# Row tiles of 64 partitions for the first product of a fused adapter and feed-forward kernel

## The chip, the cores and the metric

The kernel runs on one core of a Trainium2 chip. The metric is the device time of one execution in microseconds (us); the kernel before takes 297.78 us, the median of 3 runs (297.61 to 297.8).

## What is computed

The reference, cut to what matters (x is 8 x 256 x 1024, the adapter weights 16 x 1024 x 1024, all fp32):

```
w = weight[adapter_ids]
y = einsum('bsi,boi->bso', x, w)             # first product, one adapter per batch row
t = y[:, perm] as 16 heads of 64
t = gelu(einsum('bhd,hdm->bhm', t, up))      # 64 -> 256
t = einsum('bhm,hmd->bhd', t, down)          # 256 -> 64
out = x + t[:, unperm]
```

## The kernel before

**Precision.** The operands of the first product and of `up` are split into a high part (rounded to the matmul's fp32r format by ScalarE) and a low part (the difference, by VectorE). Three products are added: high by high, high by low, low by high.

**The first product (unit g, 32 of them).** A unit is 256 output columns of one batch row: two halves `o` of 128 columns, each contracted over 8 steps `k` of 128 rows. One step is a matmul of 128 rows by 128 weights by 512 columns (L641: high weights by x's high and low part side by side, `x_pair`) and one of 256 columns (L645: low weights by x's high part). They go in four groups of four: L641 x4, L645 x4, and again. Each matmul is preceded by its own weight load. The 512 columns lie in one bank of PSUM: columns 0 to 255 are the sum with x's high part, 256 to 511 that with its low part, and VectorE adds the two (`y_sum`, L518, once per half `o`) into `y_out`, which is written to a scratch in HBM and gathered back by the permutation. Units 0 and 1 (`first_lora_piece`, L606 and L611) run in pieces as the first data land.

**`up` and `down`.** A feed-forward unit f (32 of them) is two heads. `up_unit` (L674, L677, L680) has 64 rows of contraction for each head, so it issues pairs: rows 0 to 63 to one bank, rows 64 to 127 to another, 12 such pairs of 64 rows by 128 weights by 512 columns in a unit (six for each `m`). `down_unit` (L698) has 128 rows and tiles of 64 columns.

**Order on TensorE.** Written out by hand. The 32 first-product units come in eight quads `q` of four. Behind quad 2 come two up units; behind quads 3 to 6 come two up units, four down units and two more up units; behind quad 7 the rest of up and down, alternating. So the engine goes from the first product to `up` six times (behind quads 2 to 7), and from `up` back to the first product five times (ahead of quads 3 to 7).

**Banks.** PSUM is four tensors `ps[0..3]` of two banks each. Two of them (a set) are used by two units of the first product, the other two by the next two; `up` takes a set too (`up_banks(f, m)`), so a unit waits for the GELU or the `y_sum` that empties its banks (`gelu_done`, `y_summed`).

**Supply.** ScalarE rounds the weights of unit g+2 (`w_high`, L381, two pieces of 1.06 us) once unit g is done, VectorE subtracts (`w_low`, L490, two of 1.22 us); SyncE loads four units ahead. ScalarE and VectorE work through lists in a fixed order, in which `y_sum`, `t_low`, `x_low` and `w_low` follow each other.

Of the kernel before, what the change touches and what calls it, by code (L numbers as in the profile page):

```python
# [10 lines left out]
ALU = mybir.AluOpType  # L11
ACT = mybir.ActivationFunctionType

P = 128
B, S, D = 8, 256, 1024
NW = 16
H, DH, M = 16, 64, 256
KT = D // P
OU = 256
OT = OU // P  # L20
# [5 lines left out]
FU = H // 2  # L26
MT = M // P
HALF = KT // 2
NL = B * LPB
NF = CH * FU  # L30

# [23 lines left out]
YS, TG, SS, HS, XR = 4, 6, 2, 4, 9  # L55
# [4 lines left out]
PAIR, QUAD, LEAD = 2, 4, 2  # L60
# [17 lines left out]
def build(nc, x_cols, x_rows, x_late, w, up, down, perm, ids, out_rows, out_late):  # L78
# [3 lines left out]
    with ctx:  # L82
# [14 lines left out]
        w_hi = sb("w_hi", [P, WS, KT, OU], F32R)  # L97
        w_lo = sb("w_lo", [P, WS, KT, OU], F32R)
# [62 lines left out]
        y_summed = sem("y_summed")  # L161
# [37 lines left out]
                return ps[2 * ((p // 2 + 1) % 2) + p % 2][:, f % 2, :]  # L199
            return ps[2 * ((p + 1 - TURNS + BLOCKS) % 2)][:, f % 2, :]  # L200

        def y_bank(g, o):
            q = g // QUAD
            return ps[2 * ((q + g % QUAD // 2 + (q == LEAD)) % 2) + g % 2][:, o, :].rearrange("p (c s) -> p c s", c=2)

        def token_parts(f):

# [278 lines left out]
        def _(dve):  # L486
# [26 lines left out]
            def y_sum(g):  # L513
                if g >= YS:
                    dve.wait_ge(y_parked[g % YS], 16 * (g // YS))
                for o in range(OT):
                    dve.wait_ge(lora_done, OT * g + o + 1)
                    nc.vector.tensor_reduce(y_out[:, g % YS, o, :], y_bank(g, o).rearrange("p c s -> p s c"),  # L518
                                            mybir.AxisListType.X, ALU.add).then_inc(y_summed, 1)

            def add_x(f):
# [70 lines left out]
        @block.tensor  # L592
        def _(pe):
            def warm():
                pe.wait_ge(ones_set, 1)
                for n in range(WARM):
                    nc.tensor.matmul(ps[3][:, 1, 0:P], ones, ones, start=True, stop=True)

            def first_lora_piece(g, n):
                ks = range(*FIRST[n])  # L600
                pe.wait_ge(first_x_lo, n + 1)
                pe.wait_ge(first_w_hi[g], n + 1)
                for o in range(OT):
                    col = slice(o * P, (o + 1) * P)
                    for k in ks:
                        nc.tensor.matmul(y_bank(g, o), w_hi[:, g, k, col], x_pair[:, 0, k, :, :], start=(k == 0), stop=False)  # L606
                pe.wait_ge(first_w_lo[g], n + 1)
                for o in range(OT):
                    col = slice(o * P, (o + 1) * P)
                    for k in ks:  # L610
                        last = nc.tensor.matmul(y_bank(g, o)[:, 0, :], w_lo[:, g, k, col], x_hi[:, 0, k, :], start=False, stop=(k == KT - 1))  # L611
                    if n == PIECES - 1:
                        last.then_inc(lora_done, 1)
                if g == 0 and n == HALF_PIECE:
                    last.then_inc(first_half_done, 1)

            def lora_unit(g):
                b, ws = g // LPB, g % WS
                xs = b % XS
                if g % LPB == 0:  # L620
                    pe.wait_ge(x_lo_done, b)


                q = g // QUAD
                if q > LEAD:
                    f = PAIR * 2 * (q - LEAD - 1) + g % QUAD // 2
                    pe.wait_ge(gelu_done, MT * f + g % 2 + 1)
                elif q == LEAD:
                    pe.wait_ge(y_summed, OT * (g - QUAD + 1))
                elif q > 0:  # L630
                    pe.wait_ge(y_summed, OT * (g - 1 if g % QUAD < 2 else g - 5))
                for o in range(OT):
                    col = slice(o * P, (o + 1) * P)
                    acc = y_bank(g, o)
                    for n in range(2):
                        ks = range(n * HALF, (n + 1) * HALF)

                        if o == 0:
                            pe.wait_ge(w_hi_done, 2 * (g - PAIR) + n + 1)
                        for k in ks:  # L640
                            nc.tensor.matmul(acc, w_hi[:, ws, k, col], x_pair[:, xs, k, :, :], start=(k == 0), stop=False)  # L641
                        if o == 0:
                            pe.wait_ge(w_lo_done, 2 * (g - PAIR) + n + 1)
                        for k in ks:
                            last = nc.tensor.matmul(acc[:, 0, :], w_lo[:, ws, k, col], x_hi[:, xs, k, :], start=False, stop=(k == KT - 1))  # L645
                    last.then_inc(lora_done, 1)

            def up_unit(f):
                p, ts = f // PAIR, f % SS

                behind_quad = p == 0 or p % 2 == 1 and p <= TURNS
                q = (p + 1) // 2 + LEAD
                if f == 0:
                    pe.wait_ge(up_lo_done, len(UP_UNITS))
                if behind_quad:

                    pe.wait_ge(y_summed, OT * (QUAD * q + 2 * (f % 2 + 1)))
                elif f % 2 == 1:

                    pe.wait_ge(added, f - 1 if p < TURNS else f - 3)  # L660
                pe.wait_ge(t_lo_done, f + 1)
                for m in range(MT):
                    col = slice(m * P, (m + 1) * P)


                    if not behind_quad and f % 2 == 0:
                        pe.wait_ge(gelu_done, MT * (f - 1) + m + 1)
                    if not behind_quad and f % 2 == 1 and p > TURNS:
                        pe.wait_ge(gelu_done, MT * (f - 3) + m + 1)
                    acc = up_banks(f, m)  # L670

                    for h in range(2):
                        own = slice(h * DH, (h + 1) * DH)
                        nc.tensor.matmul(acc[:, h, :], up_hi[own, f % FU, col], t_hi[own, ts, :], start=True, stop=False)  # L674
                    for h in range(2):
                        own = slice(h * DH, (h + 1) * DH)
                        nc.tensor.matmul(acc[:, h, :], up_hi[own, f % FU, col], t_lo[own, ts, :], start=False, stop=False)  # L677
                    for h in range(2):
                        own = slice(h * DH, (h + 1) * DH)
                        last = nc.tensor.matmul(acc[:, h, :], up_lo[own, f % FU, col], t_hi[own, ts, :], start=False, stop=True)  # L680
                    last.then_inc(up_done, 1)

            def down_unit(f):
                if f == 0:
                    pe.wait_ge(down_in, 16)

                p = f // PAIR
                if f % PAIR == 0:
                    if p < TURNS - 1:
                        pe.wait_ge(gelu_done, MT * PAIR * (p // 2 * 2 + 1) + p % 2 + 1)  # L690
                    else:
                        pe.wait_ge(gelu_done, MT * PAIR * (p + 1) + 1 if p + 1 < PAIRS else MT * NF)
                for n, tok in enumerate(token_parts(f)):
                    acc = down_place(f, n)
                    for m in range(MT):
                        pe.wait_ge(gelu_done, MT * f + m + 1)
                        for h in range(2):
                            last = nc.tensor.matmul(acc[h * DH:(h + 1) * DH, :], down_sb[:, 2 * (f % FU) + h, m, :],  # L698
                                                    hidden[:, f % HS, m, h, tok], start=(m == 0), stop=(m == MT - 1))
                    last.then_inc(down_done, 1)  # L700

            warm()
            for n in range(PIECES):
                for g in range(PAIR):
                    first_lora_piece(g, n)
            for q in range(QUADS):
                k = block_behind(q)
                for g in lora_of(q):
                    if g >= PAIR:
                        lora_unit(g)  # L710
                if k:
                    for f in units(2 * k - 1):
                        up_unit(f)
                    for f in units(2 * k - 2):
                        down_unit(f)
                    for f in units(2 * k - 1):
                        down_unit(f)
                if k is not None:
                    for f in units(2 * k):
                        up_unit(f)  # L720
            for p in range(TURNS, PAIRS):
                for f in units(p):
                    up_unit(f)
                for f in units(p - 1):
                    down_unit(f)
            for f in units(PAIRS - 1):
                down_unit(f)
# [37 lines left out]
```

## Time and profile before

| | |
|---|---|
| time, median of 3 runs | 297.78 us (297.61 to 297.8) |
| span of the profiled execution | 296.1 us |
| what lies around the span (the median less the span) | 1.7 us |
| TensorE matmul busy | 290.6 us, 98% |
| TensorE weight load busy | 215.0 us, 73% |
| VectorE, ScalarE, GpSimd busy | 61%, 54%, 33% |
| matmuls | 1694 |

The profiled execution has no time of its own beside its span, so the median of the runs stands for it. Busy time of TensorE counts overlapping matmuls once. The profiler's record of one matmul is longer than the slot it occupies (a matmul of 512 columns is recorded with 395 ns while the next starts 233 ns later), so what a matmul costs is read from start to start.

### The profile page before, as it was taken

What the parts mean: (1) busy time and instruction counts of PE and PEld (TensorE: products, weight loads), DVE (VectorE), ACT (ScalarE), POOL (GpSimd) and SP (SyncE); (2) the same over time, 40 slices, a digit from 0 to 9 for tenths busy, and PEclk for the clock granted to TensorE, in tenths of its full rate; (3) what the DMA queues carried; (4) which work ended last, traced back from release to release, by engine and by line L of the source; (5) the groups of instructions that cost most, each with busy time, mean ns of one, the idle gap of its engine ahead of it and who ended that gap; (6) DMA issues with size and microseconds to landing.
All of it is one profiled execution on the core that took longest, in us unless ns stands there. A gap on an engine that the chain in (4) does not pass through costs nothing.

```text
span 296.1 us, 4358 instructions
## 1 busy us (share of the span) xinstructions
PE 290.6 (98%) x1694; PEld 215.0 (73%) x1694; DVE 179.2 (61%) x211; ACT 159.9 (54%) x179; POOL 98.8 (33%) x92
## 2 busy tenths in 40 slices
PE   8999999999999999999999999999999999999994
PEld 7788888888888838886488855888468885444441
DVE  3599679589778455973658726685446523343333
ACT  5655453466764368344584265822853207777750
POOL 4000000068552007860527007702473405222234
PEclk9999999999999999999999999999999999999999
DMA  7999999999988947799576973876752864421335
GB/s 206 363 402 421 395 421 422 366 320 375 394 328 277 378 153 197 281 360 406 212 249 196 345 311 114 312 237 199 244 191 83 286 185 122 128 71 71 144 142 212
DMA packets 23699, 77.87 MB, mean 263 GB/s; under 512 B 2688, under 2 KB 11264, under 8 KB 18816
## 3 DMA queue, kind: packets, MB, share of 16 engines
q1 hardware_dynamic: 7056, 43.39, 39.3%
q0 software_dynamic: 7488, 25.18, 24.7%
q10 hardware_dynamic: 9136, 9.05, 8.8%
q8 instruction: 13, 0.21, 0.3%
q14 instruction: 6, 0.05, 0.1%
HBM read 60.82 MB, written 16.78 MB: 262 GB/s over the span
## 4 chain that ended last, share of the span: by engine, by line
PE 95%; DMA 2%; SPq 1%; POOL 1%; issue 0%; DVE 0%; ACT 0%; POOLq 0%; DVEq 0%
PE ps L641 38%; PE ps L645 19%; PE ps L698 19%; PE ps L674 6%; PE ps L677 5%; PE ps L680 5%; PE ps L606 2%; DMA w_raw<-w 2%; PE ps L611 1%; POOL out_late L319 1%; SPq L223 1%; SPq L251 0%; DVE w_raw L528 0%; ACT w_hi L429 0%; POOLq L361 0%
## 5 line engine op out<-in xcount | busy, mean ns | idle before, releaser
L641 PE MATMUL ps<-x_pair,w_hi 128*128 128x512 f32 x480 | 131.5, 395 | 0.0
L381 ACT ACTIVATE w_hi<-w_raw 128x1024 fp32r<-128x1024 f32 x58 | 58.3, 1056 | 62.8 <-PE ps L645 51.6
L415 ACT ACTIVATE hidden<-ps 128x1024 f32<-128x1024 f32 x64 | 61.6, 1028 | 55.1 <-PE ps L680 47.1
L641 PEld LDWEIGHTS ps<-x_pair,w_hi 128*128 128x128 f32 x480 | 82.0, 189 | 12.8 <-issue 1.8
L645 PEld LDWEIGHTS ps<-x_pair,w_lo 128*128 128x128 f32 x480 | 73.6, 189 | 10.2
L490 DVE TENSOR_TENSOR w_lo<-w_raw,w_hi 128x1024 fp32r<-128x1024 f32 x60 | 71.0, 1222 | 11.8 <-ACT w_hi L381 10.7
L645 PE MATMUL ps<-x_pair,w_lo 128*128 128x256 f32 x480 | 76.3, 281 | 0.0
L292 POOL DMA_INDIRECT t_raw<-y_rows,idx x32 | 34.9, 1090 | 115.1 <-DMA y_rows<-y_out 82.4
L518 DVE TENSOR_REDUCE y_out<-ps 128x256 f32<-128x512 f32 x64 | 42.8, 685 | 24.5 <-PE ps L645 23.0
L698 PE MATMUL ps<-hidden,down_sb 128*64 128x512 f32 (+1 forms) x264 | 57.4, 583 | 0.0
L510 DVE TENSOR_TENSOR t_lo<-t_raw,t_hi 128x512 fp32r<-128x512 f32 x32 | 21.7, 694 | 47.9 <-ACT t_hi L405 42.5
L698 PEld LDWEIGHTS ps<-hidden,down_sb 128*64 128x64 f32 x264 | 18.0, 137 | 34.0 <-issue 30.9
L298 POOL DMA_INDIRECT rows<-x_rows,idx x16 | 22.6, 1414 | 14.7 <-PE ps L645 10.8
L674 PE MATMUL ps<-t_hi,up_hi 64*128 64x512 f32 x128 | 27.0, 418 | 0.0
L311 POOL DMA_INDIRECT out_rows<-rows,idx x16 | 20.1, 1254 | 18.2 <-DVE rows L528 14.9
L677 PE MATMUL ps<-t_lo,up_hi 64*128 64x512 f32 x128 | 25.1, 389 | 0.0
L680 PE MATMUL ps<-t_hi,up_lo 64*128 64x512 f32 x128 | 25.0, 387 | 0.0
L405 ACT ACTIVATE t_hi<-t_raw 128x512 fp32r<-128x512 f32 x32 | 19.9, 642 | 0.9 <-DMA t_raw<-y_rows,idx 0.9
L674 PEld LDWEIGHTS ps<-t_hi,up_hi 64*128 64x128 f32 x128 | 12.0, 184 | 11.4 <-issue 7.3
L499 DVE TENSOR_TENSOR x_pair<-x_raw,x_pair 128x2048 fp32r<-128x2048 f32 x7 | 16.0, 2292 | 4.9 <-ACT x_pair L387 4.7
L528 DVE TENSOR_TENSOR rows<-ps,rows 128x512 f32<-128x512 f32 x16 | 11.0, 690 | 10.3 <-PE ps L698 10.3
L307 POOL DMA_INDIRECT w_raw<-x_late,idx x8 | 8.3, 1042 | 23.1 <-DVE w_lo L490 17.0
(29 smaller groups left out, 119.4 us busy)
## 6 DMA issues: line engine op xcount, KB each, us to landing
w_raw<-w SPq DMA_DIRECT2D x29, 1024.0 KB
y_rows<-y_out ACTq DMA_DIRECT2D x32, 256.0 KB
x_raw<-x_cols SPq DMA_DIRECT2D x7, 1024.0 KB
w_raw<-w SPq DMA_DIRECT2D x4, 256.0 KB, 5.0
w_raw<-w SPq DMA_DIRECT2D x2, 512.0 KB, 7.7
hidden<-up SPq DMA_DIRECT2D x1, 1024.0 KB, 12.3
down_sb<-down SPq DMA_DIRECT2D x1, 1024.0 KB, 12.3
w_raw<-w SPq DMA_DIRECT2D x2, 384.0 KB, 6.9
```

Source lines behind the costliest of these rows:

```text
L292: nc.gpsimd.indirect_dma_start(t_raw[:, f % TG, :], None, y_rows[0:D * (chunk + 1), :], rows_of(f)).then_inc(t_in[f % TG], 16)
L298: nc.gpsimd.indirect_dma_start(row_place(f), None, x_rows, rows_of(f)).then_inc(rows_in[f % XR], 16)
L381: nc.scalar.activation(w_hi[:, g % WS, k, :], w_raw[:, g % WRAW, k, :], ACT.Copy).then_inc(w_hi_done, 1)
L415: nc.scalar.activation(hidden[:, f % HS, m, :, :], up_banks(f, m)[:, :, :], ACT.Gelu).then_inc(gelu_done, 1)
L490: nc.vector.tensor_tensor(w_lo[:, g % WS, k, :], w_raw[:, g % WRAW, k, :], w_hi[:, g % WS, k, :].bitcast(F32), ALU.subtract).then_inc(w_lo ...
L518: nc.vector.tensor_reduce(y_out[:, g % YS, o, :], y_bank(g, o).rearrange("p c s -> p s c"), mybir.AxisListType.X, ALU.add).then_inc(y_summ ...
L641: nc.tensor.matmul(acc, w_hi[:, ws, k, col], x_pair[:, xs, k, :, :], start=(k == 0), stop=False)
L645: last = nc.tensor.matmul(acc[:, 0, :], w_lo[:, ws, k, col], x_hi[:, xs, k, :], start=False, stop=(k == KT - 1))
L674: nc.tensor.matmul(acc[:, h, :], up_hi[own, f % FU, col], t_hi[own, ts, :], start=True, stop=False)
L677: nc.tensor.matmul(acc[:, h, :], up_hi[own, f % FU, col], t_lo[own, ts, :], start=False, stop=False)
L680: last = nc.tensor.matmul(acc[:, h, :], up_lo[own, f % FU, col], t_hi[own, ts, :], start=False, stop=True)
L698: last = nc.tensor.matmul(acc[h * DH:(h + 1) * DH, :], down_sb[:, 2 * (f % FU) + h, m, :], hidden[:, f % HS, m, h, tok], start=(m == 0), s ...
```

## The change

For units 2 to 31 each step of 128 rows becomes two row tiles of 64 rows, as in `up`, each with its own bank. To fit two banks per half unit, x's high and low part are no longer side by side but two matmuls of 256 columns that accumulate into the same columns. A step has then six matmuls of 64 rows by 128 weights by 256 columns (three pairs), each with a weight load, in place of one of 512 and one of 256 columns. VectorE now adds the two row tiles rather than the high and the low sum. Where both halves `o` of a unit share the two banks (units that are not `by_half`), `y_sum` is one instruction over 1024 elements after the whole unit; where each half has banks of its own and two units share those (`by_half`: the last two units of quads 3 to 7), it stays one per half. The waits of `lora_unit` and `up_unit` follow the new places.

```
-        def y_bank(g, o):
+        def by_half(g):
+            return g // QUAD > LEAD and g % QUAD >= PAIR
+        def y_tiles(g, o):
+            n, m = (o, g % 2) if by_half(g) else (g % 2, o)
+            return ps[2 * y_set(g) + n][:, :, m * S:(m + 1) * S]
...
             def y_sum(g):
...
+                if g >= PAIR and not by_half(g):
+                    dve.wait_ge(lora_done, OT * (g + 1))
+                    nc.vector.tensor_reduce(y_out[:, g % YS, :, :].rearrange("p o s -> p (o s)"),
+                                            ps[2 * y_set(g) + g % 2][:, :, :].rearrange("p r t -> p t r"),
+                                            mybir.AxisListType.X, ALU.add).then_inc(y_summed, OT)
+                    return
...
             def lora_unit(g):
...
+                    if by_half(g):
+                        if g % 2 == 0:
+                            pe.wait_ge(gelu_done, MT * f + o + 1)
+                        else:
+                            pe.wait_ge(y_summed, OT * (g - 1) + o + 1)
...
                         for k in ks:
-                            nc.tensor.matmul(acc, w_hi[:, ws, k, col], x_pair[:, xs, k, :, :], start=(k == 0), stop=False)
+                            for c in range(2):
+                                for r in range(2):
+                                    own = slice(r * ROWS, (r + 1) * ROWS)
+                                    nc.tensor.matmul(acc[:, r, :], w_hi[own, ws, k, col], x_pair[own, xs, k, c, :],
+                                                     start=(k == 0 and c == 0), stop=False)
...
                         for k in ks:
-                            last = nc.tensor.matmul(acc[:, 0, :], w_lo[:, ws, k, col], x_hi[:, xs, k, :], start=False, stop=(k == KT - 1))
+                            for r in range(2):
+                                own = slice(r * ROWS, (r + 1) * ROWS)
+                                last = nc.tensor.matmul(acc[:, r, :], w_lo[own, ws, k, col], x_hi[own, xs, k, :],
+                                                        start=False, stop=(k == KT - 1))
...
             def up_unit(f):
...
-                if behind_quad:
-                    pe.wait_ge(y_summed, OT * (QUAD * q + 2 * (f % 2 + 1)))
+                if behind_quad and f % 2 == 0:
+                    pe.wait_ge(y_summed, OT * (QUAD * q + PAIR))
+                elif behind_quad:
+                    pass
...
+                    if behind_quad and f % 2 == 1:
+                        pe.wait_ge(y_summed, OT * (QUAD * q + 3) + m + 1 if q > LEAD else OT * (QUAD * q + 3 + m))
```

## Rows read from the trace of the kernel before

**Rows 1.** The page: busy shares, granted clock, chain of work that ended last.

```profile
span 296.1 us, 4358 instructions
PE 290.6 (98%) x1694; PEld 215.0 (73%) x1694; DVE 179.2 (61%) x211; ACT 159.9 (54%) x179; POOL 98.8 (33%) x92
...
PEclk9999999999999999999999999999999999999999
...
PE ps L641 38%; PE ps L645 19%; PE ps L698 19%; PE ps L674 6%; PE ps L677 5%; PE ps L680 5%; PE ps L606 2%; DMA w_raw<-w 2%; PE ps L611 1%; POOL out_late L319 1%; SPq L223 1%; SPq L251 0%; DVE w_raw L528 0%; ACT w_hi L429 0%; POOLq L361 0%
```

**Rows 2.** The page's groups: line engine op, shapes, count | busy us, mean ns.

```profile
L641 PE MATMUL ps<-x_pair,w_hi 128*128 128x512 f32 x480 | 131.5, 395 | 0.0
L645 PE MATMUL ps<-x_pair,w_lo 128*128 128x256 f32 x480 | 76.3, 281 | 0.0
```

**Rows 3.** Waits, all engines: who waited for whom, us, times, longest.

```profile
ACT w_hi L381 <- PE ps L645: 51.6, 18, 3.6
...
ACT w_hi L381 <- DMA w_raw<-w: 1.7, 2, 1.0
...
PE ps L597 <- DVE rows L543: 1.1, 1, 1.1
...
PE ps L606 <- ACT w_hi L429: 0.4, 1, 0.4
```

**Rows 4.** Chain in order of time, one unit apart (start us, us).

```profile
119.30 0.93 PE ps L641 x4
...
124.91 0.93 PE ps L641 x4
```

**Rows 5.** Timeline of PE from the first product into up (start us, us).

```profile
98.56 0.63 PE L645 MATMUL ps<-x_pair,w_lo 128*128 128x256 f32 x4
99.03 1.09 PE L641 MATMUL ps<-x_pair,w_hi 128*128 128x512 f32 x4
99.96 0.64 PE L645 MATMUL ps<-x_pair,w_lo 128*128 128x256 f32 x4
100.52 0.50 PE L674 MATMUL ps<-t_hi,up_hi 64*128 64x512 f32 x2
100.86 0.40 PE L677 MATMUL ps<-t_lo,up_hi 64*128 64x512 f32 x2
```

**Rows 6.** Timeline of PE from up into the first product.

```profile
110.82 0.40 PE L677 MATMUL ps<-t_lo,up_hi 64*128 64x512 f32 x2
...
113.11 0.39 PE L680 MATMUL ps<-t_hi,up_lo 64*128 64x512 f32 x2
113.43 1.20 PE L641 MATMUL ps<-x_pair,w_hi 128*128 128x512 f32 x4
114.47 0.39 PE L645 MATMUL ps<-x_pair,w_lo 128*128 128x256 f32 x2
```

**Rows 7.** Timeline after a wait in up: weight loads (PEld) and matmuls (PE).

```profile
250.76 0.19 PEld L674 LDWEIGHTS ps<-t_hi,up_hi 64*128 64x128 f32 x2 [0.32 <-DVE w_raw L528]
250.76 0.50 PE L674 MATMUL ps<-t_hi,up_hi 64*128 64x512 f32 x2
250.87 0.19 PEld L677 LDWEIGHTS ps<-t_lo,up_hi 64*128 64x128 f32 x2
```

**Rows 8.** Timeline of weight loads beside the matmuls of rows 5.

```profile
98.91 0.54 PEld L641 LDWEIGHTS ps<-x_pair,w_hi 128*128 128x128 f32 x3
```

**Rows 9.** Timeline at the first matmul of unit 0, behind a wait.

```profile
6.09 0.19 PEld L606 LDWEIGHTS ps<-x_pair,w_hi 128*128 128x128 f32 x1 [0.26 <-DVE x_pair L534]
6.12 0.47 PE L606 MATMUL ps<-x_pair,w_hi 128*128 128x512 f32 x1
```

**Rows 10.** TensorE's sequencer at line L696, window 101 to 105 us (min/median/max ns).

```profile
L696 PEldq EVENT_SEMAPHORE  x2: 51/728/1406, 101.5 to 103.5; - x2
```

**Rows 11.** Timeline of VectorE in units 13 to 15, and PE into unit 15.

```profile
90.26 1.28 DVE L518 TENSOR_REDUCE y_out<-ps 128x256 f32<-128x512 f32 x2
91.46 2.34 DVE L490 TENSOR_TENSOR w_lo<-w_raw,w_hi 128x1024 fp32r<-128x1024 f32 x2
93.72 0.68 DVE L518 TENSOR_REDUCE y_out<-ps 128x256 f32<-128x512 f32 x1
...
94.34 0.64 PE L645 MATMUL ps<-x_pair,w_lo 128*128 128x256 f32 x4
94.82 0.63 PE L641 MATMUL ps<-x_pair,w_hi 128*128 128x512 f32 x2
```

More of the change, by code:

```diff
@@ L28 @@
 HALF = KT // 2
+ROWS = P // 2
 NL = B * LPB
@@ L200, in down_bank, with y_set, first_bank @@
             return ps[2 * ((p + 1 - TURNS + BLOCKS) % 2)][:, f % 2, :]
-        def y_bank(g, o):
+        def y_set(g):
             q = g // QUAD
-            return ps[2 * ((q + g % QUAD // 2 + (q == LEAD)) % 2) + g % 2][:, o, :].rearrange("p (c s) -> p c s", c=2)
+            return (q + g % QUAD // 2 + (q == LEAD)) % 2
+        def by_half(g):
+            return g // QUAD > LEAD and g % QUAD >= PAIR
+        def first_bank(g, o):
+            return ps[2 * y_set(g) + g % 2][:, o, :].rearrange("p (c s) -> p c s", c=2)
+        def y_tiles(g, o):
+            n, m = (o, g % 2) if by_half(g) else (g % 2, o)
+            return ps[2 * y_set(g) + n][:, :, m * S:(m + 1) * S]
         def token_parts(f):
@@ L515, in y_sum @@
                     dve.wait_ge(y_parked[g % YS], 16 * (g // YS))
+                if g >= PAIR and not by_half(g):
[4 more added lines that the diff above has]
+                    return
                 for o in range(OT):
+                    parts = first_bank(g, o) if g < PAIR else y_tiles(g, o)
                     dve.wait_ge(lora_done, OT * g + o + 1)
-                    nc.vector.tensor_reduce(y_out[:, g % YS, o, :], y_bank(g, o).rearrange("p c s -> p s c"),
+                    nc.vector.tensor_reduce(y_out[:, g % YS, o, :], parts.rearrange("p c s -> p s c"),
                                             mybir.AxisListType.X, ALU.add).then_inc(y_summed, 1)
@@ L605, in first_lora_piece @@
                     for k in ks:
-                        nc.tensor.matmul(y_bank(g, o), w_hi[:, g, k, col], x_pair[:, 0, k, :, :], start=(k == 0), stop=False)
+                        nc.tensor.matmul(first_bank(g, o), w_hi[:, g, k, col], x_pair[:, 0, k, :, :], start=(k == 0), stop=False)
                 pe.wait_ge(first_w_lo[g], n + 1)
@@ L610, in first_lora_piece @@
                     for k in ks:
-                        last = nc.tensor.matmul(y_bank(g, o)[:, 0, :], w_lo[:, g, k, col], x_hi[:, 0, k, :], start=False, stop=(k == KT - 1))
+                        last = nc.tensor.matmul(first_bank(g, o)[:, 0, :], w_lo[:, g, k, col], x_hi[:, 0, k, :], start=False, stop=(k == KT - 1))
                     if n == PIECES - 1:
@@ L624, in lora_unit @@
                 q = g // QUAD
-                if q > LEAD:
-                    f = PAIR * 2 * (q - LEAD - 1) + g % QUAD // 2
+                f = PAIR * 2 * (q - LEAD - 1) + g % QUAD // 2
+                if q > LEAD and not by_half(g):
                     pe.wait_ge(gelu_done, MT * f + g % 2 + 1)
@@ L629, in lora_unit @@
                     pe.wait_ge(y_summed, OT * (g - QUAD + 1))
-                elif q > 0:
+                elif 0 < q < LEAD:
                     pe.wait_ge(y_summed, OT * (g - 1 if g % QUAD < 2 else g - 5))
@@ L633, in lora_unit @@
                     col = slice(o * P, (o + 1) * P)
-                    acc = y_bank(g, o)
+                    acc = y_tiles(g, o)
+                    if by_half(g):
[3 more added lines that the diff above has]
+                            pe.wait_ge(y_summed, OT * (g - 1) + o + 1)
                     for n in range(2):
```

## The prediction

> **What bounds the kernel now.** The page comes first. Matmuls are busy for 98% of the span at the full granted clock (all slices show 9 and over, the 2.4 GHz level), and the chain of work that ended last lies on TensorE for 95%: 38% of it on L641 and 19% on L645, the two matmuls of the changed units [rows 1]. Then the waits: TensorE waited for other engines only 1.1 and 0.4 us, both at the start, while ScalarE waited 51.6 us for the first product and only 1.7 us for weights from DMA [rows 3]. So every ns of a TensorE slot counts in full, and supply follows TensorE. The groups give 480 steps (30 units x 2 halves x 8) [rows 2]. The price of a step is read from start to start: a unit takes 124.91 - 119.30 = 5.61 us in the chain [rows 4], that is 16 steps of 0.3508 us. It splits into 0.93 / 4 = 0.2325 us for 512 columns and 0.47 / 4 = 0.1175 for 256 [rows 5].
>
> **What the change takes away: changes of tile shape.** The first product has 128-row tiles, `up` 64-row tiles. Into `up`, four L645 take 100.52 - 99.96 = 0.56 us where they take 0.47 within a unit, and the first pair then takes 100.86 - 100.52 = 0.34 where the later ones take 0.23: 0.09 + 0.11 = 0.20 us [rows 5, 6]. Back again, the last pair takes 113.43 - 113.11 = 0.32 (0.09 more) and four L641 take 114.47 - 113.43 = 1.04 (0.11 more): 0.20 us too [rows 6]. After the change both have tiles of 64 rows and 128 columns. Six changes into `up` and five back go, one comes new between unit 1 and unit 2: 10 x 0.20 = 2.0 us less, all on TensorE's path, since there is nothing that it then waits for (below). The shapes of `down` stay and so do their costs. TensorEngine Tiling (Array Packing), Key Properties, in the Trainium skill says that a change of the tiling mode drains the array; by that the 0.09 goes in any case, and the trace agrees.
>
> **What the change reprices: the step.** It removes a 512-column and a 256-column matmul and adds three pairs of 64 rows by 256 columns; matmuls go from 1694 to 1694 + 4 x 480 = 3614. No row shows a 64-row pair of 256 columns. The nearest are these.
> - The 64-row pair of 512 columns in `up`: from 110.82 to 113.11 us there are ten pairs, 0.229 us each [rows 6]. Its two matmuls start together and run side by side: one slot for two. Against 0.2325 for one 128-row matmul of 512 columns it is 1.5% shorter.
> - The 128-row matmul of 256 columns: 0.1175 [rows 5].
>
> Lower bound: half of 0.229, 0.1145 us, if a pair costs by its columns alone. Then a step is 0.3435, 0.0073 less, x 480 = 3.5 us less. A floor under it is the weight load: behind a wait the next loads start 0.11 us after the first [rows 7], so no slot goes below 0.11 (0.33 a step, 10.0 us less); I see no reason to get there, since the 256-column slot of now, with one such load, is 0.1175 and not 0.11.
> Upper bound: a pair has two weight loads and two matmuls, four instructions in a slot, twice what any stretch of before needs. After the one kind of wait that empties the queue, a matmul follows its load 0.03 us later (6.09, 6.12) [rows 9]. If that is the pace of handing out instructions, a slot is 4 x 0.03 = 0.12 us, a step 0.36, 0.0092 more, x 480 = 4.4 us more.
> Value taken: 0.117, the present 256-column slot less most of the 1.5% that row pairs save at 512 columns, since length is the same and only the rows differ. A step is 0.351: x 480 = 0.1 us more, so nothing. Splitting the 512 columns gives back what pairs save.
>
> **Could the two weight loads in a slot be one after the other?** That would be 0.22 us a slot and is excluded: after a wait both loads of a pair and both matmuls start at 250.76, and the next pair of loads starts at 250.87, as long as one load takes [rows 7].
>
> **Weight loads and matmuls overlap already.** The timeline shows L641's loads starting at 98.91, while L645 still runs, and one slot apart after that [rows 8, 5]. TensorE: Matmul & The Clock Gate, Part 3, in the Trainium skill says that a weight load overlaps a running matmul only when its row group differs. By that rule the 128-row stream would pay each load in full, and a change to two row tiles would save far more than I count: 0.11 us for each of 960 loads, over 100 us. Here the trace is against it, and it gets no chance: 0.1175 us for 256 columns leaves no room for an exposed load of 0.11.
>
> **VectorE and the waits that move.** `y_sum` of a whole unit is one instruction in place of two, which took 1.28 us together when run one after the other [rows 11]; I count about 1.2 for the one. It starts only after the whole unit, so the sum lands about 0.5 us later than the second half's did. Behind it stand `w_low` of two units ahead and, on ScalarE, the store of `y_out` with the next `w_high`: both have a unit of 5.6 us. The tight one is new: the first half of unit 15 waits until VectorE has summed the first half of unit 14, since they share banks. That sum ends at 93.72 + 0.68 = 94.40 and unit 15 begins at 94.82 [rows 11]: 0.42 us of cover. Quad 3 starts 0.20 us sooner, and VectorE's list ahead of it shortens by 0.1: cover 0.3, cost 0. With slots of 0.1145 the three units before it shorten by 0.35 us more and the cover is just gone, for 0.1 us, once. In later quads VectorE is further ahead. DMA needs no more than now, and ScalarE waits for it 1.7 us in all [rows 3].
>
> **Sum.** 297.8 (the median of the runs; span 296.1, around it 1.7) + 0.1 - 2.0 = 295.9 us, 0.6% faster. About 0.2% is what a measurement of this kernel can tell from no change, 0.6 us.
>
> **Rivals.**
> - *Instructions are handed out too slowly* (the other side). The price is above: 297.8 + 4.4 - 2.0 = 300.2 us. It decides from the point where it eats 2.0 us: a step of 0.355, a slot of 0.1183, 0.0296 us an instruction. For it: the 0.03 of [rows 9]. Against it: at L696 the sequencer's wait that began at 101.5 us and took 1.406 us ended at 102.9, and its next wait, two down units and so 32 instructions further if it is the one ahead of f = 2, began at 103.5: 0.6 / 32 = 0.019 us each [rows 10]. But the trace doesn't name which instruction that wait stands ahead of. Chance 0.20. TensorE: Matmul & The Clock Gate, Part 1, in the Trainium skill gives about 62 ns for a matmul where hardware decoding is off and a floor of 25 ns where it is on; by the first, an estimate, a slot would be 0.124, a step 0.372 and the time 306 us; no row shows which holds.
> - *Row pairs lose something at 256 columns*: two loads of 0.11 us, a few ns apart, have to fit a slot of 0.117, and any slip shows. Slot 0.119 to 0.120: 1.9 us and more, less 2.0; 298 to 300 us. For it: no stretch of before has loads that dense. Chance 0.15.
> - *Cost by columns alone*, a slot of 0.1145: 297.8 - 3.5 - 2.0 + 0.1 = 292.4 us. For it: pairs are shorter at 512 columns than single matmuls. Against it: 256 columns now cost 0.1175, more than half of 0.2325. Chance 0.20.
> - *TensorE starts to wait* for `y_sum` or GELU, 0.3 us in each of five quads, 1.5 us: 297.4 us. Chance 0.05.
>
> The forecast has 0.40: slots of 0.1155 to 0.1183, 293.6 to 297.8 us. Range over the cases: 292.2 to 302.2 us, which takes in both bounds of the slot and leaves out some 0.08 on either side. Faster by over 0.2%: 0.20 of the columns case, 0.29 of the forecast's: 0.49. Within 0.2%: 0.17 (the forecast's upper end, waits, part of the denser loads). Slower: 0.34.
>
> **What would show it.** The start-to-start time of pairs in a unit (0.117; 0.12 or more says hand-out or loads, 0.1145 says columns); the last slot before `up` and the first in it like any other (else the 2.0 us are wrong); TensorE's waits still near 1.5 us in all; a single `y_sum` of about 1.2 us. The prediction fails most easily by the slot: 0.001 us in it is 1.4 us of time.

## The result, and the profile after

The changed kernel takes 300.31 us (median of 4 runs, 299.84 to 300.7) beside 297.69 us for the kernel before (4 runs, 297.53 to 297.8): a ratio of 1.0085, 95% interval 1.0071 to 1.0099. It is 0.85% slower; the forecast was 295.9 us, faster. The profiled execution took 299.84 us, the shortest of the four, and has a span of 298.0 us. In this document medians take in all runs of a kernel, while ratios leave out the runs more than 1.5% above its fastest (two of six of v1, five of twelve of v3).

The page of the kernel after, its busy shares and its chain, answers to [rows 1]:

```profile
span 298.0 us, 8180 instructions
PE 292.2 (98%) x3614; PEld 240.2 (81%) x3614; DVE 177.0 (59%) x191; ACT 159.9 (54%) x179; POOL 100.9 (34%) x92
...
PEclk9999999999999999999999999999999999999999
...
PE ps L673 39%; PE ps L680 19%; PE ps L739 18%; PE ps L715 5%; PE ps L718 5%; PE ps L721 5%; PE ps L629 3%; PE ps L634 1%; DMA w_raw<-w 1%; DVE w_raw L551 1%; POOL out_late L335 1%; SPq L239 1%; ACT w_hi L445 0%; POOLq L377 0%; SPq L267 0%
```

TensorE is as full as before, at the same granted clock, and the same two products set the end. Its busy time has grown by 1.6 us. So the loss is in how long TensorE takes for the work, not in waits. TensorE's waits confirm it (who waited for whom, us, times, longest), as in [rows 3]:

```profile
PE ps L620 <- DVE rows L566: 1.1, 1, 1.1
...
PE ps L629 <- ACT w_hi L445: 0.7, 1, 0.7
```

The chain in order of time (start us, us) shows the step; it answers to [rows 4]:

```profile
114.33 0.95 PE ps L673 x16
115.28 0.48 PE ps L680 x8
...
120.08 0.96 PE ps L673 x16
```

A unit takes 120.08 - 114.33 = 5.75 us (the next one 5.76), 16 steps of 0.360 us, where it was 0.3508. Eight pairs take 0.96, so a pair's slot is 0.120 us. That is 480 x (0.360 - 0.3508) = 4.4 us more.

TensorE's timeline from the first product into `up` and back, in the kernel after, answers to [rows 5] and [rows 6]:

```profile
100.98 0.64 PE L680 MATMUL ps<-x_pair,w_lo 64*128 64x256 f32 x8
101.46 0.40 PE L715 MATMUL ps<-t_hi,up_hi 64*128 64x512 f32 x2
101.69 0.40 PE L718 MATMUL ps<-t_lo,up_hi 64*128 64x512 f32 x2
...
113.94 0.39 PE L721 MATMUL ps<-t_hi,up_lo 64*128 64x512 f32 x2
114.17 1.11 PE L673 MATMUL ps<-x_pair,w_hi 64*128 64x256 f32 x16
115.12 0.64 PE L680 MATMUL ps<-x_pair,w_lo 64*128 64x256 f32 x8
```

The last four pairs of a unit take 101.46 - 100.98 = 0.48 us, like any other, and the first `up` pair 0.23, where they took 0.56 and 0.34. Back again, the last `up` pair takes 0.23 in place of 0.32 and the first eight pairs 0.95, no more than later ones. Nothing of either seam is left. So both 0.20 us costs are gone: ten changes, 2.0 us.

4.4 - 2.0 = 2.4 us more; the medians differ by 2.6, and the wait for `w_hi` at the start has grown by 0.3. The spans of the two traces differ by 1.9 only, since the start took less in this execution: unit 2 begins at 17.98 us, in the kernel before at 18.70. The quads show the account without it: each of quads 3 to 7 takes 23.03 us in place of 22.64, and 64 steps at 0.0092 more, less the 0.20 of two half seams, are 0.39.

VectorE at units 13 to 15 (timeline) answers to [rows 11]:

```profile
90.79 1.22 DVE L534 TENSOR_REDUCE y_out<-ps 128x512 f32<-128x1024 f32 x1
...
94.19 0.68 DVE L541 TENSOR_REDUCE y_out<-ps 128x256 f32<-128x512 f32 x1
```

And TensorE into unit 15:

```profile
95.70 1.12 PE L673 MATMUL ps<-x_pair,w_hi 64*128 64x256 f32 x16
```

The one-instruction sum takes 1.22 us. The sum that unit 15 waits for ends at 94.19 + 0.68 = 94.87, so the new wait has 95.70 - 94.87 = 0.83 us of cover: more than thought, because TensorE is later.

### The profile page after: what moved, and what is told of

Read it like the earlier page. It is cut to its first block, busy times and chain, and to the rows that moved or that the text cites. A ratio compares the mean times of both kernels' runs of the same rounds, so it can differ in the third digit from the quotient of the medians.

```text
span 298.0 us, 8180 instructions
## 1 busy us (share of the span) xinstructions
PE 292.2 (98%) x3614; PEld 240.2 (81%) x3614; DVE 177.0 (59%) x191; ACT 159.9 (54%) x179; POOL 100.9 (34%) x92
## 4 chain that ended last, share of the span: by engine, by line
PE 95%; DMA 1%; DVE 1%; POOL 1%; SPq 1%; issue 0%; ACT 0%; POOLq 0%; DVEq 0%
PE ps L673 39%; PE ps L680 19%; PE ps L739 18%; PE ps L715 5%; PE ps L718 5%; PE ps L721 5%; PE ps L629 3%; PE ps L634 1%; DMA w_raw<-w 1%; DVE w_raw L551 1%; POOL out_late L335 1%; SPq L239 1%; ACT w_hi L445 0%; POOLq L377 0%; SPq L267 0%
## 5 line engine op out<-in xcount | busy, mean ns | idle before, releaser
L673 PE MATMUL ps<-x_pair,w_hi 64*128 64x256 f32 x1920 | 134.9, 280 | 0.0
L673 PEld LDWEIGHTS ps<-x_pair,w_hi 64*128 64x128 f32 x1920 | 124.0, 188 | 0.5
L680 PE MATMUL ps<-x_pair,w_lo 64*128 64x256 f32 x960 | 77.2, 280 | 0.0
L308 POOL DMA_INDIRECT t_raw<-y_rows,idx x32 | 35.5, 1108 | 116.9 <-DMA y_rows<-y_out 101.4
L680 PEld LDWEIGHTS ps<-x_pair,w_lo 64*128 64x128 f32 x960 | 66.1, 188 | 0.0
L534 DVE TENSOR_REDUCE y_out<-ps 128x512 f32<-128x1024 f32 x20 | 24.4, 1221 | 17.0 <-PE ps L680 17.0
L314 POOL DMA_INDIRECT rows<-x_rows,idx x16 | 24.3, 1518 | 13.3 <-PE ps L680 9.1
L541 DVE TENSOR_REDUCE y_out<-ps 128x256 f32<-128x512 f32 x24 | 16.2, 687 | 18.3 <-PE ps L680 18.3
L715 PE MATMUL ps<-t_hi,up_hi 64*128 64x512 f32 x128 | 26.3, 407 | 0.1
```

Source lines behind the costliest of these rows:

```text
L308: nc.gpsimd.indirect_dma_start(t_raw[:, f % TG, :], None, y_rows[0:D * (chunk + 1), :], rows_of(f)).then_inc(t_in[f % TG], 16)
L314: nc.gpsimd.indirect_dma_start(row_place(f), None, x_rows, rows_of(f)).then_inc(rows_in[f % XR], 16)
L534: nc.vector.tensor_reduce(y_out[:, g % YS, :, :].rearrange("p o s -> p (o s)"), ps[2 * y_set(g) + g % 2][:, :, :].rearrange("p r t -> p t r"),
L673: nc.tensor.matmul(acc[:, r, :], w_hi[own, ws, k, col], x_pair[own, xs, k, c, :], start=(k == 0 and c == 0), stop=False)
L680: last = nc.tensor.matmul(acc[:, r, :], w_lo[own, ws, k, col], x_hi[own, xs, k, :], start=False, stop=(k == KT - 1))
```

## The experiments

What needs a cause is the slot: why 0.120 us for 256 columns, and is it the split, the row tiles, the weight loads or the number of instructions?

### e1, e2, e3: fewer columns, shorter loads, both

From the kernel after. e1 has 192 moving columns instead of 256, e2 weight loads of 64 columns instead of 128, e3 both; the edit of e3:

```diff
-nc.tensor.matmul(acc[:, r, :], w_hi[own, ws, k, col], x_pair[own, xs, k, c, :],
+few = slice(0, S if k == 0 and c == 0 else 192)
+part = slice(o * P, o * P + (P if k == 0 and c == 0 else 64))
+out = slice(0, P if k == 0 and c == 0 else 64)
+nc.tensor.matmul(acc[out, r, few], w_hi[own, ws, k, part], x_pair[own, xs, k, c, few],
...
-last = nc.tensor.matmul(acc[:, r, :], w_lo[own, ws, k, col], x_hi[own, xs, k, :],
+wide, much = (P, S) if k == KT - 1 else (64, 192)
+last = nc.tensor.matmul(acc[0:wide, r, 0:much], w_lo[own, ws, k, o * P:o * P + wide], x_hi[own, xs, k, 0:much],
```

> The changed kernel with 192 of the 256 columns in all matmuls of the first product in units 2 to 31, except each half unit's first high pair and last low pair (left out: the other columns' work). Theory A, the slot of a pair is set by its weight loads (load start to next matmul 0.117 us, plus 0.003): the slot stays 0.120 us and the time near 300 us. Theory B, instructions are handed out every 0.03 us: 0.120 as well. Theory C, the columns of a row pair set it: 0.120 x 192 / 256 = 0.090 us, and about 1260 slots x 0.030 = 38 us less.

> The changed kernel with weight loads of 64 instead of 128 columns in the same matmuls, 256 moving columns (left out: half of the output columns). Theory A (loads): a load is half as long (about 0.053 us less), so the slot falls to what 256 columns need by themselves, about 0.1145 us (half of a 512-column pair's 0.229), minus nothing else; two changes of tile shape per half unit come on top. Theory B (hand-out, four instructions in a slot): 0.120 still. Theory C (columns): 0.120 still.

> Both at once: weight loads of 64 columns and 192 moving columns, still two loads and two matmuls in a slot. Theory A (loads) and C (columns): about 0.086 to 0.090 us. Theory B (hand-out at 0.03 us an instruction): the slot can't go below 0.120. This run decides B.

Their times of one run each (316.27, 308.99 and 301.45 us, beside 297.56 for the kernel before) say little about the slot, for in all three TensorE stood still in places and its granted clock fell. In e1 these pauses are 4.1 us in `up` and 7.5 us in 21 pieces inside the first product. In e1, the page's slices of the granted clock:

```profile
PEclk9999999997789999988999999979999999999999
```

and TensorE's timeline in `up` behind quad 2:

```profile
77.03 0.79 PE L719 MATMUL ps<-t_hi,up_hi 64*128 64x512 f32 x2 [4.14 <-issue]
77.59 0.66 PE L722 MATMUL ps<-t_lo,up_hi 64*128 64x512 f32 x2
78.02 0.66 PE L725 MATMUL ps<-t_hi,up_lo 64*128 64x512 f32 x2
```

TensorE had stood still for 4.1 us, and then a pair of 512 columns takes 78.02 - 77.59 = 0.43 us in place of 0.23: the lower level, 1.2 GHz, until 81.4 us. `up` had come early for its rows: TensorE was through with the first product at 72.9 us, 2 us sooner than in the kernel before, and ScalarE's `t_hi` waited for the gathering DMA until 75.53 us. TensorE ran ahead of what feeds it and paid twice.

The slot is read from an undisturbed stretch. TensorE's timelines, e1 first:

```profile
169.68 1.13 PE L676 MATMUL ps<-x_pair,w_hi 64*128 64x192 f32 x16
170.57 0.71 PE L684 MATMUL ps<-x_pair,w_lo 64*128 64x192 f32 x8
```

Then e2:

```profile
168.36 1.09 PE L676 MATMUL ps<-x_pair,w_hi 64*64 64x256 f32 x16
169.27 0.65 PE L684 MATMUL ps<-x_pair,w_lo 64*64 64x256 f32 x8
```

And e3:

```profile
169.58 0.88 PE L676 MATMUL ps<-x_pair,w_hi 64*64 64x192 f32 x16
170.30 0.57 PE L684 MATMUL ps<-x_pair,w_lo 64*64 64x192 f32 x8
```

Eight pairs take 0.89 us in e1 (0.111 a slot), 0.91 in e2 (0.114) and 0.72 in e3 (0.090). With fewer columns the slot stops at 0.111, the time of one 128-column load in [rows 7]; with shorter loads it stops at 0.114, half of an `up` pair of 512 columns (0.229); with both it goes to 0.090. There are four instructions in each of these slots, so one can be handed out every 0.0225 us or faster, in a stretch of this length. The rival "instructions are handed out too slowly" needed 0.03 and falls. What is left is odd: 0.111 with full loads, 0.114 with all columns, but 0.120 where both are full length.

### e5: loads of 96 columns

The edit is that of e2 with 96 for 64.

> The changed kernel with weight loads of 96 of 128 columns, except each half unit's first high and last low pair (left out: a quarter of the output columns). Theory D: 0.1067 + 96 x 0.000104 = 0.1167 us a slot (0.120 at 128, 0.1135 at 64). If a load costs a fixed time whatever its length, 0.120.

303.75 us, one run, beside 297.76. TensorE's timeline:

```profile
83.16 1.09 PE L675 MATMUL ps<-x_pair,w_hi 64*128 64x256 f32 x16
84.09 0.63 PE L683 MATMUL ps<-x_pair,w_lo 64*96 64x256 f32 x8
```

The eight pairs of the first row take 0.93 us, a slot of 0.116 (the first pair has full loads, the row names only that form). That lies between the 0.114 of 64 columns and the 0.120 of 128. So a load costs a little of a slot long before it would fill it. The expectation for a cost that grows with the load's length was 0.1167, and for a fixed one 0.120; the first came near. The total says nothing of it, since the trace has 2.3 us of pauses inside the first product.

### e8: the split alone, in the kernel before

```diff
-nc.tensor.matmul(acc, w_hi[:, ws, k, col], x_pair[:, xs, k, :, :], start=(k == 0), stop=False)
+for c in range(2):
+    nc.tensor.matmul(acc[:, c, :], w_hi[:, ws, k, col], x_pair[:, xs, k, c, :],
+                     start=(k == 0 and c == 0), stop=False)
```

> The kernel before with one thing of the change alone: L641 split into two 128-row matmuls of 256 columns (x's high and low part), each with its own weight load, into the columns they had. Theory D (a fixed cost for each load): a step is 3 x 0.1175 to 3 x 0.120 = 0.3525 to 0.360 us, so 298.5 to 302.1 us, and the split rather than the row tiles makes the change slow. Theory E (row pairs are the cause): 0.3508 and 297.7 us.

303.01 us (302.71 to 303.51, 4 runs), ratio 1.0165, interval 1.0114 to 1.0215. Its chain:

```profile
119.01 0.96 PE ps L642 x8
...
120.45 0.96 PE ps L642 x8
```

Matmuls of all 128 rows, one load and one matmul to a slot, and the slot is 0.120 us again (0.96 / 8). The step is (120.45 - 119.01) / 4 = 0.360, so the split costs 480 x 0.0092 = 4.4 us with no row tile in the program. It has the costs of tile shapes as well, since it still changes between 128 and 64 rows, and its list of waits has one of 0.6 us that the kernel before has not (L646 for `w_lo`).

297.76 + 4.4 + 0.6 = 302.8, measured 303.01. And the kernel after is 2.7 us faster than this one: 2.6 of it are the 2.0 us of the ten changes and that wait. This run decides: the slot of 0.120 belongs to 256-column matmuls in a row, not to pairs.

### v1: row tiles without the split

The complement. Pairs of 512 columns and of 256, as L641 and L645 were; each half of a unit then has four parts in two banks, and `y_sum` adds four parts:

```diff
-for c in range(2):
-    for r in range(2):
-        own = slice(r * ROWS, (r + 1) * ROWS)
-        nc.tensor.matmul(acc[:, r, :], w_hi[own, ws, k, col], x_pair[own, xs, k, c, :],
-                         start=(k == 0 and c == 0), stop=False)
+for r in range(2):
+    own = slice(r * ROWS, (r + 1) * ROWS)
+    nc.tensor.matmul(acc[:, r, :], w_hi[own, ws, k, col], x_pair[own, xs, k, :, :],
+                     start=(k == 0), stop=False)
...
+nc.vector.tensor_reduce(y_out[:, g % YS, o, :], y_tiles(g, o).rearrange("p r (c s) -> p s r c", c=2),
+                        mybir.AxisListType.XY, ALU.add).then_inc(y_summed, 1)
```

> Row tiles without the split: the high product as pairs of 512 columns (x's high and low part side by side), the low product as pairs of 256, two banks for each half unit, so a unit takes a whole set of four banks and y_sum adds four parts. Theory D (a slot costs its columns, 1 / 2.4 GHz each, plus what its weight loads take from it, 0.013 us for loads of 128 columns, however many columns move): a step is 0.229 + 0.120 = 0.349 us against 0.3508, 480 x 0.0018 = 0.9 us less, with the ten changes of tile shape saved (2.0 us) 294.8 us, plus whatever TensorE waits for y_sum, which is twice the work on VectorE. Theory E (a 64-row pair of 256 columns is slow in itself or the saved changes of shape were never saved): 297.7 or slower.

302.89 us (300.29 to 305.24, 6 runs), ratio 1.0114, interval 1.0058 to 1.0170. TensorE's timeline inside a quad:

```profile
124.11 1.09 PE L658 MATMUL ps<-x_pair,w_hi 64*128 64x512 f32 x8
...
125.51 1.09 PE L658 MATMUL ps<-x_pair,w_hi 64*128 64x512 f32 x8
```

Four steps take 125.51 - 124.11 = 1.40 us, a step of 0.350: that of the kernel before, with twice the instructions. Row pairs neither save nor cost anything in a slot. The 0.229 us of a pair in `up` is not 1.5% that pairs save at 512 columns, as the prediction had it. The changes of tile shape are saved here too: three of quads 3 to 7 take 22.43 to 22.48 us where all took 22.64.

The run still lost 4.8 us of span, outside the slots, where the expectation was 294.8 us. The largest part, 1.75 us, is `up` behind quad 2, where VectorE is late with its longer sums; TensorE stands still for 1.2 us twice, the second time by this wait:

```profile
PE ps L700 <- DVE y_out L534: 1.2, 1, 1.2
```

Quads 4 and 6 take 22.87 and 23.63 us, with pauses inside them. At the start and late in the run there is another 1.6 us. The rest is at the seam behind a quad:

```profile
211.82 1.22 DVE L534 TENSOR_REDUCE y_out<-ps 128x256 f32<-128x1024 f32 x1 [1.23 <-PE ps L665]
213.55 1.94 ACT L427 ACTIVATE hidden<-ps 128x1024 f32<-128x1024 f32 x2 [5.53 <-DVE y_out L534]
213.87 0.40 PE L706 MATMUL ps<-t_hi,up_lo 64*128 64x512 f32 x2
214.63 0.65 PE L724 MATMUL ps<-hidden,down_sb 128*64 128x512 f32 x2 [0.35 <-ACT hidden L427]
```

The sum of half a unit takes 1.22 us in place of 0.68; ScalarE's GELU stands in its program behind the store of that sum, and `down` starts 214.63 - 213.87 = 0.76 us after the last `up` pair, not 0.32 as in the kernel before. The `up` stretches behind quads 3 to 7 take 3.01 to 3.59 us in place of 2.94.

### v2, v3: a candidate from these two

If the split is the loss and the tile shapes the gain, row pairs of full width in units 12 to 31 alone should keep the gain and spare VectorE in the crowded first part. v3 also moves one store on ScalarE:

```diff
 for f in units(2 * k - 1):
     gelu(f)
+    if f % 2 == 0:
+        y_park(QUAD * q + 3)
     t_high(f + PAIR)
```

> The kernel before, with row tiles of 64 rows for units 12 to 31 alone (the quads between two up stretches) and without the split: one pair of 512 columns and one of 256 a step, four banks of parts, summed by VectorE in two instructions of 1.22 us. Units 2 to 11 stay as before. Theory (the split cost the 4.4 us, the tile shapes give 0.20 us at each change, VectorE's longer sums eat part of it): quads at 22.43 us as in the undisturbed ones of the version with row pairs everywhere, where they were 22.64 before; up stretches behind them 3.00 instead of 2.94 because the last sum comes late; up stretches ahead of them 2.85. Per quad 0.24 us less, less up to 0.1 where down then waits for GELU; five quads: 0.7 to 1.2 us, so 296.5 to 297.1 us beside 297.7. Rival (VectorE's doubled sums are felt in every quad): quads or up stretches 0.4 us and more longer, 298.5 us and more.

> The same kernel with one instruction moved on ScalarE: the store of the last y_out of a quad comes behind the first GELU of the up stretch instead of ahead of it, so that GELU does not wait until VectorE has summed that unit. Theory: TensorE's down stretch behind that up stretch starts as early as in the kernel before (0.315 us between the last up matmul and the first down matmul or less, where the version with row pairs everywhere once took 0.756), 0.1 to 0.4 us in each of up to five quads: 295.7 to 296.9 us. Rival (ScalarE has slack there and the wait is VectorE's alone): same time as the kernel without the move, within 0.2 us.

v2: 299.47 us (298.32 to 302.25, 9 runs), ratio 1.0068, interval 1.0038 to 1.0097. v3: 300.7 us (296.72 to 303.33, 12 runs), ratio 1.0024, interval 0.9989 to 1.0058. v2 is slower than the kernel before, by 0.7%, and v3 is not shown to be faster; both missed their expectations, and v2 landed where its rival had it. In v2 `up` behind quads 3 to 7 takes 3.58, 3.12, 3.04, 3.26 and 3.01 us where it took 2.94; with the moved store, in v3, it takes 2.96, 2.94, 2.86, 3.01 and 3.01, so that part is cured. The spread of v3 is not the clock: the granted clock was 0.994 to 1.0 in all twelve runs. Its traced execution took 301.64 us, one of the longer ones. Its timeline of TensorE shows that the mechanism is there all the same:

```profile
172.26 0.63 PE L668 MATMUL ps<-x_pair,w_lo 64*128 64x256 f32 x8
172.74 0.40 PE L704 MATMUL ps<-t_hi,up_hi 64*128 64x512 f32 x2
172.97 0.40 PE L707 MATMUL ps<-t_lo,up_hi 64*128 64x512 f32 x2
...
175.28 0.39 PE L710 MATMUL ps<-t_hi,up_lo 64*128 64x512 f32 x2
175.59 0.65 PE L728 MATMUL ps<-hidden,down_sb 128*64 128x512 f32 x2
```

The slots at the seam are 0.48 / 4 and 0.23 us, none is long, and `down` follows the last `up` pair after 0.31 us. Two stretches of first product between `up` and `up` (span, busy time of PE, PEld, DVE, ACT and POOL; the last three columns are granted clock, DMA share, GB/s) show what spoils it:

```profile
113.39:137.50 24.11, 23.32 (x259) 22.14 (x257) 19.07 (x17) 10.87 (x12) 15.12 (x13) 1.00 0.90 316
150.31:172.74 22.43, 22.43 (x260) 19.60 (x257) 18.62 (x17) 10.85 (x12) 6.71 (x6) 1.00 0.83 259
```

The second quad takes 22.43 us against 22.64 before, the first 24.11. The third takes 24.72, and TensorE's timeline of it has such a place:

```profile
190.41 0.51 PE L668 MATMUL ps<-x_pair,w_lo 64*128 64x256 f32 x4 [0.84 <-issue]
```

In the middle of a run of eight (the first four start at 189.17), where the program waits for nothing, TensorE stands still ("issue": nothing that the profile shows). Instruction records of the DMA queues lie close by in time, and the kernel moves 0.29 MB of instructions where the one before moves 0.21; but the kernel after moves 0.46 MB and has no such pause. The cause stays open.

### e4, e7, e6: what a load costs in other places

e4 is the kernel before with L645 over 128 of its 256 columns; e7 is the kernel before with loads of 64 columns; e6 is v1 with loads of 64 columns. The edit of e4:

```diff
-last = nc.tensor.matmul(acc[:, 0, :], w_lo[:, ws, k, col], x_hi[:, xs, k, :], ...)
+last = nc.tensor.matmul(acc[:, 0, 0:P], w_lo[:, ws, k, col], x_hi[:, xs, k, 0:P], ...)
```

> The kernel before with the low product (L645) over 128 of its 256 columns (left out: half of that product). Theory A (loads): the 128-row slot of 256 columns is already set by its load, so with 128 columns it hardly falls, 0.115 to 0.118 us, and the time stays within 1 to 2 us of 297.7. Theory C (columns): 0.1175 falls to about 0.06 us, 960 slots... that is 480 x 0.058 = 28 us less. Theory B says nothing here (two instructions in a slot, 0.06 at least): also about 28 us less.

293.82 us, one run, beside 297.56. TensorE's timeline:

```profile
82.99 0.56 PE L645 MATMUL ps<-x_pair,w_lo 128*128 128x128 f32 x4
...
84.35 0.56 PE L645 MATMUL ps<-x_pair,w_lo 128*128 128x128 f32 x4
```

Four steps take 84.35 - 82.99 = 1.36 us (1.367 in the median of the trace), 0.340 to 0.342 a step against 0.3508. Half the columns of L645 save 0.01 us of a step, not the 0.06 that columns alone would: there is a floor under a slot with a 128-column load, near the 0.11 us of [rows 7]. In the trace the second to fourth of these slots take 0.110 to 0.113 us; the first takes 0.058, and the 512-column slot behind the four takes 0.05 more than it did.

> The kernel before with weight loads of 64 columns instead of 128 in L641 and L645 of the units from two on, except for the first of the eight hi steps and the last of the eight lo steps; half of the output columns get no sum of these steps. If the 256-column slot of a single 128-row matmul is set by its 128-column load, it falls from 0.118 towards the 0.1135 that pairs of 256 columns took with 64-column loads, and the 512-column slot stays at 0.2325: a step 0.005 us less, 2 us in all. If columns alone set it, nothing changes, 297.6 us.

297.03 us, one run, beside 297.81. A step becomes shorter:

```profile
82.48 1.08 PE L642 MATMUL ps<-x_pair,w_hi 128*64 128x512 f32 x4
...
85.24 1.08 PE L642 MATMUL ps<-x_pair,w_hi 128*64 128x512 f32 x4
```

(85.24 - 82.48) / 8 = 0.345 us, about 0.006 less, 2.8 us in 480 steps; but the time fell by 0.8 only. A wait of 1.4 us came up that was not there, in `up` for the sum of y (L676 for `y_out`); what is left of the difference one run can't settle.

> The variant with pairs of 512 columns, with weight loads of 64 columns (left out: half of the output columns). Theory D: the 512-column pair falls from 0.226 to 0.229 to 0.213 + 0.007 = 0.220 us, the 256-column pair to 0.1135. If the cost goes with the moving columns, the 512-column pair loses twice what the 256-column pair lost (0.0065): 0.213 to 0.216.

303.97 us, one run, beside 297.76; the total is again made by waits and pauses elsewhere. The timeline gives the step:

```profile
123.89 1.08 PE L659 MATMUL ps<-x_pair,w_hi 64*64 64x512 f32 x8
...
125.28 1.08 PE L659 MATMUL ps<-x_pair,w_hi 64*128 64x512 f32 x8
...
126.66 0.62 PE L659 MATMUL ps<-x_pair,w_hi 64*64 64x512 f32 x4
```

Eight steps take 126.66 - 123.89 = 2.77 us, 0.346 a step (0.345 in the median of the trace), as in e7 and 0.005 less than v1. Pairs and single matmuls gain the same from shorter loads. The 512-column slot falls to some 0.230 us in both runs, not to the 0.220 that was expected of e6: the rule that fitted 256 columns does not hold for 512.

So where long and short matmuls stand side by side, halving the loads saves some 0.003 us a slot, and the load is felt most where every slot is 256 columns: 0.006, from 0.120 to 0.114.

### v4: hi and lo by turns

The last experiment uses that. Only the order in the second half of each unit changes:

```diff
 for k in ks:
     nc.tensor.matmul(acc, w_hi[:, ws, k, col], x_pair[:, xs, k, :, :], start=(k == 0), stop=False)
+    if o == 1:
+        last = nc.tensor.matmul(acc[:, 0, :], w_lo[:, ws, k, col], x_hi[:, xs, k, :], ...)
+if o == 1:
+    continue
```

> The kernel before, with the matmuls of each unit's second half in another order: hi and lo by turns (512, 256, 512, 256 columns) in place of four of 512 and four of 256. Same instructions, same tiles, same sums; the first halves stay. In the kernel before, a slot's length depends on its neighbours: the fourth 512-column slot of a run, which the load of a 256-column matmul follows, takes 228.7 ns on the mean of 61 runs and the others 231.8 to 239.2; the first 256-column slot behind them takes 117.0 and the later ones 118.9 to 120. Theory (a slot costs by its neighbours, so loads that stand next to a 512-column matmul are hidden better): a step by turns is 0.2287 + 0.117 = 0.3457 us where it is 0.3508 now; 240 steps save 1.2 us, 296.6 us beside 297.7. Rival (the slots' spread is only the bookkeeping of one run of four, and the sum stays 0.3508): no change, 297.4 to 298.0 us. A third (loads of 256-column slots hidden worse when each follows a long one): slower.

297.17 us (12 runs, 296.95 to 298.3) beside 297.82 (17 runs), ratio 0.9974, interval 0.9949 to 1.0000. By its median it is the fastest version that leaves nothing out, by 0.26%, at the edge of what can be told. The chain, four steps by turns and four of the old order:

```profile
121.37 0.23 PE ps L641
121.60 0.12 PE ps L643
...
124.15 0.92 PE ps L641 x4
...
125.55 0.93 PE ps L641 x4
```

Eight steps by turns take 124.15 - 121.37 = 2.78 us, 0.3475 a step, against 1.40 / 4 = 0.350 in the old order: 240 x 0.0025 = 0.6 us, about what was measured and half of what was expected. In the median of the trace a 256-column slot by turns is 0.1165 us, as reckoned, but a 512-column slot is 0.231 and not 0.2287. Each of quads 3 to 7 takes 22.55 us where it took 22.64.

## Why the prediction was wrong, step by step

- **The step that failed is the value taken for the slot: "Value taken: 0.117 ... so nothing."** It measures 0.120, and 480 x 3 x 0.003 = 4.3 us is the whole error. Three readings lay behind it. First, 0.1175 was read from one group of four L645 of the kernel before. Its chain in order of time shows two kinds by turns:

```profile
120.23 0.47 PE ps L645 x4
...
121.63 0.48 PE ps L645 x4
```

That is 0.119 on the mean of the two, and the prediction's own step says 0.3508 - 0.2325 = 0.1183. Second, such a slot stands in a run of four between 512-column ones, whose first slot is short (0.117, the later ones 0.118 to 0.120); in an unbroken row it is 0.120 (e8). Third, "the 1.5% that row pairs save at 512 columns" does not exist: with 512-column pairs in the same order the step is 0.350 as before (v1).
- **"Splitting the 512 columns gives back what pairs save"**: it gives back 4.4 us, against 2.0 from the tile shapes. The split had to be priced as an edit of its own: 2 x 0.120 for 0.2325, and 0.120 for 0.1183, which is the 0.0092 of a step.
- **The rival "instructions are handed out too slowly"** named 0.12, 0.360 and 300.2 us, and 300.3 was measured. Its time came true and its mechanism did not: e8 has half as many instructions in the same slot, and e3 has as many in 0.090. A right number is no proof of the reason.
- **The rival "row pairs lose something at 256 columns"** named the right slot too and the right part, loads that are dense for the columns beside them. But it laid them on the pair; single matmuls of 128 rows lose the same (e8).
- **The lower bound** (0.1145) is near what e2 shows with loads of 64 columns, 0.114; with loads of 128 no run reached it. That it is the price of the columns alone is not shown, for no run has a slot without a load. The floor of 0.11 by the load is e1's 0.111.
- **The sums** hold but for small things: 5.61 / 16 is 0.3506, not 0.3508 (0.1 us in 480 steps), and slots of 0.1155 give 293.7 us, not 293.6.
- **The changes of tile shape: right**, 0.20 us each way, 2.0 us.
- **TensorE as the bound, no new wait: right.** The waits are 1.1 and 0.7 us where they were 1.1 and 0.4. The sum of a unit takes 1.22 us (1.2 forecast). That loads overlap the running matmuls of the same rows holds in every run: in e8 a slot of 0.120 holds a load of 0.11.
- **Still open:** why load and columns, of which 0.111 and 0.114 are measured with the other cut short, give 0.120 together.

## What to carry to other kernels

Price an edit that cuts a matmul in two by itself, and read the price of the smaller one from an unbroken row of its kind, not from a short run beside longer ones: where the load takes nearly as long as the columns, a few ns of it show in every slot, and 1440 slots make them microseconds. A difference of 1% between two forms in different surroundings is the surroundings' until one form is swapped for the other in the same place. If two products with long and short matmuls share a loop, taking them by turns is worth a trial: here it gave 0.0025 us a step in the trace, and a total at the edge of the noise (v4).

## What was not expected of the hardware

- A slot of 256 columns with a 128-column load is 0.120 us in an unbroken row, for single matmuls and pairs of row tiles alike; 0.116 with 96-column loads, 0.114 with 64; 0.111 with 192 columns and full loads; 0.090 with both cut.
- A pair of 64-row tiles costs what one 128-row matmul of the same columns costs: 1.40 us for four steps of 512 and 256 columns in either form.
- After TensorE had stood still for 4.1 us in e1, the granted clock was at the lower level, and `up` pairs took 0.43 us each where they take 0.23.
- TensorE paused in the middle of rows of matmuls that wait for nothing, for up to 1.1 us (e3) and 0.8 us (v3). Of the programs with row pairs in the first product, e1, e2, e3, e5, e6, v1, v2 and v3 show such pauses in their trace and the kernel after shows none; those with single 128-row matmuls (the kernel before, e4, e7, e8, v4) show none either.
